# A slot attention in four groups: two norms folded into weights and a diagonal matmul, the third norm spread over three engines, in a new order

## The reference, cut to what matters

```python
def _ln(x, g, b):
    mu = jnp.mean(x, axis=-1, keepdims=True)
    var = jnp.mean(jnp.square(x - mu), axis=-1, keepdims=True)
    return (x - mu) * jax.lax.rsqrt(var + LN_EPS) * g + b
x_in = _ln(x, lnkv_g, lnkv_b)
k = x_in @ wk + bk
v = x_in @ wv + bv
slots = q_mu + jnp.exp(q_logsig) * noise
for _ in range(T):                                   # T = 3
    prev = slots
    q = _ln(slots, lnq_g, lnq_b) @ wq + bq
    logits = jnp.einsum('bnd,bkd->bnk', k, q) / scale
    attn = jax.nn.softmax(logits, axis=-1) + EPS_ATTN
    attn = attn / jnp.sum(attn, axis=1, keepdims=True)
    upd = jnp.einsum('bnk,bnd->bkd', attn, v)
    slots = upd @ wu + bu + prev
    h = _ln(slots, lnm_g, lnm_b) @ w1 + b1
    slots = jax.nn.gelu(h, approximate=False) @ w2 + b2 + slots
    slots = _ln(slots + x_cls[:, None, :], lnp_g, lnp_b)
```

## Time and profile before

| What | Value |
|---|---|
| median of 3 runs | 911.91 us (911.83 to 915.03) |
| the profiled execution | 913.3 us |
| its span in the trace | 911.5 us, 18113 instructions |
| PE busy (matmuls) | 781.2 us, 86% of the span |
| DVE busy | 568.4 us, 62% |
| ACT busy | 529.7 us, 58% |
| POOL busy | 360.8 us, 40% |
| granted PE clock, mean | 0.912 |

### The profile page before, as it was taken

One profiled execution on the slowest core, in us unless ns is written; L12 is line 12 of the kernel. 1 busy time (PEld: TensorE's weight loads), 2 busy tenths in 40 slices (PEclk: granted clock), 3 DMA queues, 4 the chain that ended last, 5 costly groups with the idle time before them and its releaser, 6 DMA issues.

```text
span 911.5 us, 18113 instructions
## 1 busy us (share of the span) xinstructions
PE 781.2 (86%) x5705; PEld 645.1 (71%) x5705; DVE 568.4 (62%) x1974; ACT 529.7 (58%) x1144; POOL 360.8 (40%) x561
## 2 busy tenths in 40 slices
PE   6988799999999999989988778999968786861693
PEld 5766678878888788777876547999646565651693
DVE  1667777787776667776767653333658787874012
ACT  3665566667666677656756422333359898841462
POOL 1233444343443333332346562665413232226363
PEclk9999899999999999999989979999757979785797
DMA  8324405340701520301140044886600000001574
GB/s 263 111 66 148 143 1 168 113 178 25 267 1 30 177 57 5 99 1 33 57 161 26 25 145 135 246 248 191 215 0 1 1 1 1 1 1 39 166 200 137
DMA packets 82057, 88.54 MB, mean 97 GB/s; under 512 B 6156, under 2 KB 69852, under 8 KB 81324
## 3 DMA queue, kind: packets, MB, share of 16 engines
q1 hardware_dynamic: 78475, 80.19, 29.1%
q0 software_dynamic: 3488, 7.20, 2.2%
HBM read 69.03 MB, written 35.17 MB: 114 GB/s over the span
## 4 chain that ended last, share of the span: by engine, by line
PE 58%; DVE 20%; issue 8%; ACT 6%; POOL 5%; DMA 1%; DVEq 0%; SPq 0%; POOLq 0%; ACTq 0%
PE bank L706 6%; PE bank L1017 6%; PE bank L700 6%; DVE sb_smax L1531 4%; PE bank L733 4%; PE bank L773 3%; DVE sb_row_sum L1540 3%; PE bank L742 3%; PE bank L1025 3%; PE bank L838 3%; PE bank L758 2%; PE bank L1126 2%; PE bank L1134 2%; PE bank L715 2%; DVE sb_st_all L1857 2%
## 5 line engine op out<-in xcount | busy, mean ns | idle before, releaser
L2035 POOL TENSOR_TENSOR sb_expd<-sb_expd,sb_rden 128x512 f32<-128x512 f32 (+1 forms) x128 | 112.4, 879 | 243.5 <-DVE sb_rden L1544 243.3
L1531 DVE TENSOR_REDUCE sb_smax<-bank 128x4 f32<-128x512 f32 (+1 forms) x128 | 74.0, 578 | 66.7 <-PE bank L733 35.6
L2127 POOL TENSOR_TENSOR sb_rstd_all<-sb_rsq_all,sb_halves 128x4 f32<-128x4 f32 x44 | 45.2, 1028 | 131.6 <-DVE sb_rsq_all L1864 131.6
L1254 ACT ACTIVATE sb_expd<-sb_shifted 128x512 f32<-128x512 f32 (+1 forms) x128 | 69.7, 544 | 43.4 <-DVE sb_shifted L1534 42.4
L1540 DVE TENSOR_REDUCE sb_row_sum<-sb_expd 128x4 f32<-128x512 f32 (+1 forms) x128 | 73.0, 570 | 8.4 <-ACT sb_expd L1254 8.4
L1534 DVE TENSOR_TENSOR sb_shifted<-bank,sb_smax 128x512 f32<-128x512 f32 (+1 forms) x128 | 74.9, 585 | 4.4
L700 PE MATMUL bank<-sb_h1T,sb_watt 128*128 128x128 f32 x512 | 71.3, 291 | 4.2 <-ACT sb_h1T L1153 2.3
L700 PEld LDWEIGHTS bank<-sb_h1T,sb_watt 128*128 128x128 f32 x512 | 65.5, 204 | 6.8 <-DMA sb_watt<-att_w 2.7
L1017 PE MATMUL bank<-sb_blk_xT,sb_up_w 128*128 128x128 f32 x456 | 57.1, 275 | 0.0
L1017 PEld LDWEIGHTS bank<-sb_blk_xT,sb_up_w 128*128 128x128 f32 x456 | 54.0, 192 | 0.0
L1824 DVE TENSOR_TENSOR sb_hid<-bank,sb_hid 128x384 f32<-128x384 f32 x38 | 21.2, 558 | 51.1 <-ACT sb_hid L1302 51.1
(11 more groups left out here) (270 smaller groups left out, 2006.9 us busy)
## 6 DMA issues: line engine op xcount, KB each, us to landing
sb_up_w<-gate_up SPq DMA_DIRECT2D x38, 384.0 KB
sb_v<-v_all SPq DMA_DIRECT2D x16, 576.0 KB, 6.6
rows_b<-pad_b SPq DMA_DIRECT2D x7, 1105.0 KB, 9.8
rows_a<-pad_a SPq DMA_DIRECT2D x7, 975.0 KB, 8.0
sb_up_w<-w1b SPq DMA_DIRECT2D x23, 256.0 KB
v_all<-sb_moe_w SPq DMA_DIRECT2D x14, 308.0 KB
sb_blk_x<-rows_a SPq DMA_DIRECT2D x38, 65.0 KB, 3.3
sb_picked<-back_a SPq DMA_DIRECT2D x4, 512.0 KB, 5.5
```

The lines of the kernel that those rows point to most:

```text
L1254: act.activation(exp_of(i, s, j), shifted[:, u % 2, :, 0:n], ACT.Exp, scale=DH ** -0.5).then_inc(exp_done, 1)
L1531: dve.tensor_reduce(smax[:, u % 2, :], s_in, X, ALU.max).then_inc(max_done, 1)
L2035: pool.tensor_tensor(e, e, rden[:, u % 2, :].unsqueeze(2).broadcast_to([P, QH, n]), ALU.mult).then_inc(norm_done, 1)
```

## The change

Four things are done.

- The norms `q` and `m`: centring is a multiplication by the matrix `centring` (identity minus 1/128), and the gain a scaling of the rows of the weights, so both are multiplied into the weights once (`wq_fold`, `w1_fold`, with biases `bq_fold`, `b1_fold`). What is left is the root per token. The turn, which was a transpose of the normed slots, becomes a matmul of the slots with a diagonal matrix of the roots. POOL makes four such diagonals in one instruction (`diag_q`, `diag_m`), into `zs`. `shift_q`, `norm_q`, `shift_m` and `norm_m` are gone, other than in round 3, where `q` is made as before; `scale_q` and `scale_m` only copy.
- The norm `o`: `centre` and `slots` were eight DVE instructions. Now DVE makes the shift (`shift_o`), ACT the norm in four instructions (`norm_o`), POOL multiplies all four tiles by the row of gains in one (`gain`), DVE adds the row of biases in one (`slots`).
- `layer2` is split: `base` puts slots and constant into the bank by two matmuls of 512 columns, ahead of the gelu, and `layer2` adds the four products.
- `SLOT_STEPS` has a new table of numbers, so that all four engines have a new order.

```diff
+    "measure_o": (-1, ((1.4, 5.7, 9.9, 16.7,), (41.9, 43.4, 50.7, 57.8,), (82.9, 84.5, 91.8, 98.8,), (124.0, 125.5, 133.6, 138.8,),)),
+    "gain": (-1, ((6.3, 11.8, 17.6, 22.5,), (47.0, 52.8, 58.7, 63.6,), (88.1, 93.9, 99.7, 104.6,), (129.2, 133.2, 140.0, 145.6,),)),
...
+            t = slot_bank()
+            pe.wait_ge(fold_ready, 1)
+            pe.matmul(t[:, 0:P], wq_gain[:, :], centring[:, :], start=True, stop=True)
+            pe.matmul(t[:, P:2 * P], centring[:, :], w1_gain[:, :], start=True, stop=True)
+            pe.matmul(t[:, 2 * P:2 * P + 1], wqs, lnq_b, start=True, stop=True)
+            pe.matmul(t[:, 2 * P + 1:2 * P + 2], w1s, lnm_b, start=True, stop=True).then_inc(pre_slot_full, 1)
...
-            def turn_group(it, g, k, src=zs):
-                pe.wait_ge(z_normed[k], nth("norm_" + k, it, g))
-                for n in range(4):
-                    mm = pe.transpose(quads(bank[2 * g])[:, n, :], src[:, 4 * g + n, 0:D], eye[:, :])
+            def turn_group(it, g, k):
+
+                pe.wait_ge(diag_ready[k], nth("diag_" + k, it, g))
+                for n, b in enumerate(tiles(g)):
+                    mm = pe.matmul(quads(bank[2 * g])[:, n, :], S[:, b, :], zs[:, b, :], start=True, stop=True)
                 mm.then_inc(zT_done[k], 1)
...
+                if step == "base":
+                    pe.wait_ge(mid_ready, nth("updated", it, g))
+                    pe.wait_ge(zT_ready["m"], nth("scale_m", it, g))
+                    pe.matmul(bank[2 * g][:, :], eye[:, :], flat(S, g), start=True, stop=False)
+                    pe.matmul(bank[2 * g][:, :], eye[:, :], flat(cb2, g), start=False, stop=False)
                 if step == "layer2":
-                    pe.wait_ge(mid_ready, nth("updated", it, g))
                     pe.wait_ge(hid_ready, nth("gelu", it, g))
                     for n, b in enumerate(tiles(g)):
-                        pe.matmul(quads(bank[2 * g])[:, n, :], eye[:, :], S[:, b, :], start=True, stop=False)
-                        pe.matmul(quads(bank[2 * g])[:, n, :], eye[:, :], cb2[:, b, :], start=False, stop=False)
-                        mm = pe.matmul(quads(bank[2 * g])[:, n, :], hid[:, b, :], w2s, start=False, stop=True)
+                        mm = pe.matmul(quads(bank[2 * g])[:, n, :], hid[:, b, :], w2s, start=False, stop=(n == 3))
...
+            seen[0] += 1
+            act.wait_ge(pre_slot_full, 1)
+            act.activation(wq_fold[:, :], bank[0][:, 0:P], ACT.Copy)
+            act.activation(w1_fold[:, :], bank[0][:, P:2 * P], ACT.Copy)
+            act.activation(bq_fold[:, :], bank[0][:, 2 * P:2 * P + 1], ACT.Identity, bias=bq)
+            act.activation(b1_fold[:, :], bank[0][:, 2 * P + 1:2 * P + 2], ACT.Identity, bias=sb1_).then_inc(pre_slot_done, 1)
...
+                if step == "norm_o":
+                    act.wait_ge(shift_ready["o"], nth("shift_o", it, g))
+                    for n, b in enumerate(tiles(g)):
+                        ins = act.activation(S[:, b, :], x_sb[:, b, :] if it < 0 else quads(bank[2 * g])[:, n, :], ACT.Identity,
+                                             scale=rstd_all[:, b:b + 1], bias=nbias[:, b:b + 1])
+                    ins.then_inc(z_normed["o"], 1)
+                if step in ("scale_q", "scale_m"):
+                    k = step[-1]
+                    act.wait_ge(zT_done[k], nth("turn_" + k, it, g))
+                    act.activation(group_of(zsT, g), bank[2 * g][:, :], ACT.Copy).then_inc(zT_ready[k], 1)
...
+            dve.tensor_scalar(centring[:, :], eye[:, :], -1.0 / D, None, ALU.add)
+            dve.tensor_scalar(wq_gain[:, :], wqs, lnq_g, None, ALU.mult)
+            dve.tensor_scalar(w1_gain[:, :], w1s, lnm_g, None, ALU.mult).then_inc(fold_ready, 1)
...
-                if step == "centre":
-                    scale = es_b[:, :] if it < 0 else R["lnp_g"]
-                    src = x_sb if it < 0 else SUMS
-                    for b in tiles(g):
-                        ins = dve.scalar_tensor_tensor(S[:, b, :], row(src, b), mv_all[:, b, 0:1], scale, ALU.subtract, ALU.mult)
-                    link(ins)
+                if step == "shift_o":
+                    shifted_by(it, g, "o")
                 if step == "slots":
-                    dve.wait_ge(root_ready["o"], nth("root_o", it, g))
-                    stand()
-                    for b in tiles(g):
-                        ins = dve.scalar_tensor_tensor(S[:, b, :], S[:, b, :], rstd_all[:, b:b + 1],
-                                                       R["q_mu"] if it < 0 else R["lnp_b"], ALU.mult, ALU.add)
-                    ins.then_inc(S_ready, 1)
+                    dve.wait_ge(gain_done, nth("gain", it, g))
+                    dve.tensor_tensor(group(S, g), group(S, g), R["q_mu" if it < 0 else "lnp_b"].unsqueeze(1).broadcast_to([P, 4, D]),
+                                      ALU.add).then_inc(S_ready, 1)
...
+            def diagonal(k, g, count):
+
+                pool.wait_ge(root_ready[k], count)
+                pool.tensor_tensor(group(zs, g), eye[:, :].unsqueeze(1).broadcast_to([P, 4, P]),
+                                   rstd_all[:, 4 * g:4 * g + 4].unsqueeze(2).broadcast_to([P, 4, P]), ALU.mult).then_inc(diag_ready[k], 1)
...
+                if step == "gain":
+                    pool.wait_ge(z_normed["o"], nth("norm_o", it, g))
+                    scale = es_b[:, :] if it < 0 else R["lnp_g"]
+                    pool.tensor_tensor(group(S, g), group(S, g), scale.unsqueeze(1).broadcast_to([P, 4, D]), ALU.mult).then_inc(gain_done, 1)
```

More of the change, by code:

```diff
@@ L141 @@
[L141 to L155 removed]
+    "add": (-1, ((0.0, 2.9, 4.4, 11.4,),)),
@@ L156 @@
+    "gate": (3, ((140.2, 145.5, 149.2, 155.8,),)),
+    "gated": (3, ((140.7, 146.0, 149.7, 156.2,),)),
+    "choose": (3, ((150.1, 156.6,),)),
+    "rank": (3, ((152.4, 158.9,),)),
+    "place": (3, ((152.9, 159.4,),)),
+    "send": (3, ((161.2, 156.2, 166.3, 171.3,),)),
+    "choice_exp": (3, ((158.9,),)),
 }
@@ L161, in slot_steps @@
 def slot_steps(*names):
[L162 to L164 removed]
+    found = [(time, names.index(name), name, it, g) for name in names for it, times in enumerate(SLOT_STEPS[name][1], SLOT_STEPS[name][0])
+             for g, time in zip(ROUTING_AT.get(name, range(4)), times)]
+    return [step[2:] for step in sorted(found)]
 def streams(i):
```

154 lines of the change are left out of this document (66 added, 88 removed).

## The result

The changed kernel takes **929.07 us** (median of 4 runs, 926.85 to 931.39) against 911.87 us of the kernel before beside it: 1.018 times as long, 95% interval 1.0147 to 1.0219. It is slower, as forecast, but by 17.2 us and not by 7.0, and outside the range of 903 to 925 us. The time of rival 3 (929) came out, with other terms than rival 3 had.

What follows compares the result with a forecast made beforehand. VectorE and ScalarE, nearly full, bound the old rounds; VectorE-GpSimd hand-overs would bound the new. Folding 1.2, opening 12.85 + lock 1.3, rounds -0.9, end -7.8 + lock 0.3: +7.0, so 918.9 us (eight in ten: 903 to 925).

Steps and rivals of the forecast that it cites:

- rival 3: More lock, or TensorE long at the low clock: a round of 47 us, 929 us in all; chance 0.13.
- Engine work: Busy time in a round: VectorE to about 29.4 us, ScalarE about 27, GpSimd about 26; no engine full any more.
- The opening is where it loses: From the last vu copy to round 1: first slots no longer hidden under preparation, +12.85 us, and +1.3 for lock.
- The round is 42.3 us: One round of slot attention: bound by hand-overs between VectorE and GpSimd, 42.3 us instead of 44, before any lock.
- lock: VectorE instructions with two SBUF inputs held up beside large GpSimd products: 1.35 us a round, making it 43.6.
- With durations from the rows: Step following the new order through one round, each engine strictly in order, with instruction times from the earlier profile: 42.3 us.
- TensorE has more work per microsecond: Argument against TensorE staying long at the low clock in the rounds; no size of its own.
- Rounds together: The two full rounds: 2 x 43.6 us against 88.1 before, -0.9 us.
- The end: From measure_q of round 3 to the first scatter: 26.4 us against 34.2, -7.8 us, and +0.3 for lock.
- The fold: Folding of the weights ahead of the first context copy, on TensorE's full preparation stretch: about +1.2 us, bounds 0 and 2.5.
- Rival 1: Relief of VectorE and ScalarE decides: a round of 37.1 us, 897.3 us in all; chance of faster 0.23.
- The slower verdict: Whole kernel slower by more than 0.5%: chance 0.55, from 0.42 for the forecast itself and 0.13 for slower still.

Runs made afterwards that it cites:

- e1: Changed kernel with the first slots' normings between ScalarE's vu copies and their VectorE steps and measure_q ahead of the first maximum; 917.06 us.
- e13: e12 with every diagonal and gain on GpSimd replaced by a 128x4 power, so its output is not the reference's; 905.73 us.
- e12: Changed kernel with the edit of e1 plus unused TensorE matmuls, one ahead of turn_m of group 3, three ahead of update of group 0; 912.9 us.
- e7: Kernel before the change with one unused 128x512 matmul ahead of turn_q and one ahead of logits of group 2; 914.72 us.

## Why the prediction was right and wrong

**Engine work: right.** Diagonals took 1.04 us (1.07 taken), gains 1.27 (1.28), `slots` 0.69 unlocked; VectorE 31.2 us in a round (29.4), ScalarE 27.9 (27), GpSimd 26.1 (26).

**"The opening is where it loses": right.** +15.1 us against 12.85 + 1.3, by the mechanism named, and e1 takes 13.8 of them away.

**"The round is 42.3 us", a chain of hand-overs: right as a chain, wrong as a round.** At the full clock and without large products it took 42.05 us (e13). With the products it took 43.95 (e12): 1.9 more, some 1.6 of it lock, where I took 1.35. So 43.6 was a good forecast of a round at the full clock.

**"With durations from the rows": this step failed.** I entered every TensorE piece of the two rounds at its high-level duration, though the earlier trace rows gave 0.84 and 0.85 for the rounds of before, and the earlier trace rows had 1.99 beside 1.10. The low level cost 3.9 us a round. Rows 1 did not say that the low stretch was harmless; it was so, with VectorE and ScalarE full, for the half of it that e7 took away. My change to the bound, from engines to hand-overs, put TensorE's turns, updates and logits into the chain, and with that its clock. The change was priced with a chain and the clock with an average of the old kernel. "TensorE has more work per microsecond" was the argument against rival 3; its busy time is 37.7 of 47.9 us (33.7 of 44.0 before), part of which is the low level itself, and it did not help: 3.6 us of nothing preceded the second fall.

**Rounds together: +7.6 us** against -0.9; these 8.5 us are the larger part of the miss of 10.2.

**The end: -4.3 us** against -7.5. The large products cost 1.9 us (29.9 - 28.0), not 0.3: two variances took 0.92, a shift 1.11, and a power 1.51. Without them 28.0 are left (e13) where I had 26.4. VectorE waits 1.98 us for the gate of group 2 before choosing, and that chain (shift, `norm_q`, turn, `gate`) was missing from my sum.

```profile
822.75 0.92 DVE L1880 SCALAR_TENSOR_TENSOR sb_rsq_all<-sb_mv_all,sb_eps 128x4 f32<-128x4 f32 x1
828.76 1.11 DVE L1886 SCALAR_TENSOR_TENSOR sb_nbias<-sb_mv_all,sb_rstd_all 128x4 f32<-128x4 f32 x1 [1.23 <-POOL sb_rstd_all L2134]
835.33 0.19 DVE L1939 TENSOR_TENSOR sb_logits<-bank,sb_rows 128x32 f32<-128x32 f32 x1 [1.98 <-PE bank L1116]
```

**The fold: not settled.** From its first matmul to the last `vu` copy the preparation took 31.5 us, and 28.95 before. But in e7, which has no fold, it took 32.4 (635.8 to 668.2 us). The start of the preparation moved between 634.8 and 639.9 us from profile to profile. A term of 1.2 us can't be read out of that.

**The rivals.** Rival 3 had both causes and, at 47 us, nearly the round, with 0.13. Clock and lock both cost more than in the forecast, but the clock carried it: rival 3 had 1.8 us a round for the clock and 3 for the lock, and the runs show 3.9 and some 1.6. That its 929 was met to 0.1 us is luck: its rounds and its end were too short (47 for 47.85, 26.7 for 29.9), its opening (52.7, as its sum puts 3.4 us there too) 2.6 us too long, and the time up to the last `vu` copy 2.4. Rival 1 (a round of 37 us) was far off: even without lock and at the full clock the round is 42 us. The slower verdict had 0.55, rightly; the range should have reached to rival 3, since a known fall of the clock is a condition to be priced and not a mishap.

## What to carry to other kernels

When a change takes load off full engines, ask what the new chain runs through, and price each engine in it at the state it will be in: here TensorE's low clock cost 3.9 us a round after, and next to nothing before in the half that was tried. A step that is moved to another engine also takes that engine's place in the program: the normings of the first slots behind the last copy cost the opening 13.8 us, and putting them between the copies gave that back. A step that is moved to shorten one wait also moves the places where an engine stands idle, as with `base`: what looked like a gain of 1.8 us made TensorE's clock fall elsewhere and cost 2.3.
